# Two-layer graph attention: layer 1's first chunk in two parts of columns, a 13-operation epilogue, and the last chunk of layer 0 finished in GpSimd's order

## What is computed

```python
# layer 0: E are the 64-wide entity embeddings
scores = (x @ W0 @ a1)[:, None] + (E @ W0 @ a2)[None, :]
e = where(adj > 0, leaky(scores, 0.2), -9e15)
x = layernorm(x + elu(softmax(e, axis=1) @ E + x))
# layer 1: the same mask, and the new x is key and value too
wh = x @ W1
e = where(adj > 0, leaky((wh @ a_src)[:, None] + (wh @ a_dst)[None, :], 0.01), -1e9)
x = layernorm(x + softmax(e, axis=1) @ wh + bias)
```

## Time and profile before

| | |
|---|---|
| median of 3 runs | 660.34 us (659.3 to 661.42) |
| the profiled execution: its own time, its span | 659.63 us, 657.8 us |
| mean granted TensorE clock over the span | 0.961 |
| busy share of the span, TensorE matmul / VectorE / ScalarE / GpSimd | 79% / 86% / 79% / 29% |

### The profile page before, as it was taken

How to read it: one execution, slowest core, us unless ns; L and a number is a source line. 1 busy time by engine, 2 the same in 40 slices (tenths; PEclk the granted TensorE clock), 3 DMA queues, 4 the chain that set the end, 5 groups by cost and what they waited for, 6 DMA issues and landing times.

```text
span 657.8 us, 14211 instructions
## 1 busy us (share of the span) xinstructions
PE 517.0 (79%) x6034; PEld 230.6 (35%) x6035; DVE 567.6 (86%) x727; ACT 516.8 (79%) x593; POOL 188.1 (29%) x144
## 2 busy tenths in 40 slices
...
DVE  3898988999899898888467889989998998899685
ACT  0856998899999996988676318979997899699673
...
PEclk9999999999999899999999757999999999999997
...
GB/s 156 326 352 338 292 298 207 273 255 251 158 259 275 249 119 288 130 130 2 73 2 19 1 33 1 1 33 1 1 10 33 1 1 33 1 1 18 1 17 9
DMA packets 18631, 76.46 MB, mean 116 GB/s; under 512 B 6552, under 2 KB 8776, under 8 KB 10376
## 3 DMA queue, kind: packets, MB, share of 16 engines
...
q0 software_dynamic: 256, 0.80, 0.5%
...
q10 hardware_dynamic: 752, 0.13, 0.1%
...
## 4 chain that ended last, share of the span: by engine, by line
PE 28%; DVE 23%; ACT 21%; issue 18%; DMA 5%; POOL 4%; SPq 1%; POOLq 0%; ACTq 0%; DVEq 0%
ACT Pm L620 15%; PE acc L940 15%; DVE junk L726 11%; PE zps L983 8%; DVE zps L820 8%; DMA adj_in<-in_adj 5%; PE acc L947 4%; ACT zps L612 2%; ACT v L513 2%; SPq L354 1%; POOL tAB L412 1%; ACT u_row L529 1%; DVE tot L761 0%; POOL rstd L471 0%; POOL o L409 0%
## 5 line engine op out<-in xcount | busy, mean ns | idle before, releaser
L620 ACT ACTIVATE Pm<-zps,ebias 128x1024 f32<-128x1024 f32 (+1 forms) x320 | 293.4, 933 | 77.0 <-DVE zps L820 67.9
L726 DVE CUSTOM_DVE_ANT_0 junk<-v,u_row 128x2048 int8<-128x2048 int8 (+3 forms) x136 | 305.4, 2266 | 3.3 <-ACT v L513 3.2
L983 PE MATMUL zps<-D,v 128*128 128x128 bf16 x2048 | 173.7, 225 | 55.8 <-DVE D L748 28.7
L983 PEld LDWEIGHTS zps<-D,v 128*128 128x128 fp8e4 x2048 | 118.8, 99 | 216.5 <-ACT zps L612 92.0
L820 DVE SCALAR_TENSOR_TENSOR zps<-S_row,tau_col,zps 128x1024 f32<-128x1024 f32 (+1 forms) x135 | 141.2, 1052 | 52.4 <-PE zps L983 49.6
L612 ACT ACTIVATE zps<-S_row,ntau_col 128x1024 f32<-128x1024 f32 (+1 forms) x185 | 177.4, 959 | 5.4
L940 PE MATMUL acc<-Pm,X 128*32 128x512 f32 (+2 forms) x1280 | 146.5, 530 | 21.4 <-ACT Pm L620 18.1
L940 PE MATMUL acc<-Pm,VE 128*32 128x512 f32 (+2 forms) x1280 | 147.9, 535 | 15.7 <-ACT Pm L620 7.8
L402 POOL TENSOR_TENSOR tAB<-flag,totW 128x520 f32<-128x520 f32 (+1 forms) x8 | 11.1, 1388 | 300.8 <-ACT totW L539 160.9
L947 PE MATMUL acc<-Pm,ones 128*32 128x256 f32 (+1 forms) x1280 | 87.5, 346 | 0.0
L947 PEld LDWEIGHTS acc<-Pm,ones 128*32 128x32 f32 x1280 | 43.3, 114 | 71.4 <-issue 62.0
...
## 6 DMA issues: line engine op xcount, KB each, us to landing
...
```

Source lines behind the costliest of these rows:

```text
L620: a.activation(Pm[:, k % PB, 0:R(C) * P], zps[:, buf("step", k), 0:R(C) * P], ACT.Exp, bias=ebias[:, int(seeded(k)), J:J + 1])\
L726: d.tensor_tensor_reduce(out=junk[:, at % 2, 0:cols.stop - cols.start], in0=v_bytes[:, rt, cols], in1=u_row[:, cols], scale=1.0, scalar=-3 ...
L983: last = t.matmul(zps[:, buf("step", k), r * P:(r + 1) * P], v[:, chunks[C][1] + r, J * P:(J + 1) * P], D[:, C % 2, r, :], start=(r * P % ...
```

## The change

**Two parts of columns.** Chunk 5 (`NC`) now runs its steps 0 to 27 with a diagonal and constants that know only the first 28 column tiles, which chunks 0 to 3 of layer 0 produce. Steps 28 to 31 use a second diagonal, made during chunk 5 from chunk 4's new rows. The two parts have sums of their own in `acc`, are projected apart, and are weighed and added in chunk 5's epilogue. Layer 1's constants come from bounds on the scores (norms of the weight vectors, worked out in chunk 0) in place of the measured extremes.

```diff
+    KNOWN = JT - WIDTHS[0][-1]
+    SPREAD = (NC - 2, NC - 1)
...
+                second = C == NC and J >= KNOWN
+                first, end = J == KNOWN * second, J == JT - 1 or (C == NC and J == KNOWN - 1)
...
+            def second_diagonals():
+                row_terms(NC, slice(len(segments(NC)) - 1, len(segments(NC))))
+                write_diagonals(NC, PART)
+                link(d.tensor_copy(g_parts[:, 1, :], g8[:, 0:PART]))
+                link(d.tensor_tensor(um_known[:, :], um_known[:, :], um8[:, 0:PART], ALU.max))
+                write_flags(NC, um_known[:, :])
+                link(d.tensor_tensor(g_least[:, :], g_parts[:, 0, :], g_parts[:, 1, :], ALU.min))
...
+            if C == NC:
+                eng.wait_ge(weights_done, 1)
+                link(ns.tensor_tensor(o[:, 0:2 * n, :], o[:, 0:2 * n, :],
+                                      part_weight[:, :].unsqueeze(2).broadcast_to([P, 2 * n, F1]), ALU.mult))
+                link(ns.tensor_tensor(o[:, 0:n, :], o[:, 0:n, :], o[:, n:2 * n, :], ALU.add))
```

```diff
-SEEDS = ((29, 28, 28, 16, 12), (28, 18, 18, 10, 0))
+SEEDS = ((29, 28, 28, 16, 26), (26, 18, 18, 10, 0))
...
-    SAVE_ACC, PROJECT, SAVE_O, TOTALS_W, RECIPROCAL = 1, 3, 4, 5, 7
-    AFTER_WIDE = dict(elu=11, sums=14, squares=18, scores=24, rows=26)
-    AFTER_LAST = dict(elu=10, sums=13, squares=17, scores=21, rows=22)
-    IN_LAYER_1 = dict(sums=14, squares=19)
+    SAVE_ACC, PROJECT, SAVE_O, TOTALS_W = 1, 3, 4, 5
+    AFTER_WIDE = dict(reciprocal=7, elu=10, sums=13, squares=17, scores=22, rows=25)
+    IN_LAST = dict(reciprocal=6, elu=9, sums=13, squares=17, scores=21, rows=23)
...
+    IN_FIRST = dict(reciprocal=6, elu=8, sums=10, squares=13, scores=15, rows=17, maxima=19, second=21)
+    IN_LAYER_1 = dict(reciprocal=7, sums=13, squares=18)
...
+    EARLY = (4, 5, 7, 8, 9, 10, 11, 12, 14, 15, 18, 19, 22, 24)
...
-                if C == NC - 1:
-                    for n in range((Q - 2) * R(NC), (Q - 1) * R(NC)):
-                        row_max(NC, n, n % R(NC), n // R(NC))
-                    epilogue(dve, d, link, C, sums, squares, None, scores)
-                    dve.wait_ge(uS_ready, NC + 1)
-                    ext_out(EXT_BOTH)
-                    u_diagonals(uS[:, 0, 0:R(C)], R(C))
-                    ext_max(EXT_BOTH)
-                    ext_in(EXT_BOTH)
-                    t_scalars(1)
-                    s_scalars(1)
-                    for n in range((Q - 1) * R(NC), Q * R(NC)):
-                        row_max(NC, n, n % R(NC), n // R(NC))
-                    diagonals(NC)
```

```diff
-                ns.tensor_scalar(tAf, tBf, 0.0, -3.0e38, ALU.min, ALU.max).then_inc(min_done, 1)
-                eng.wait_ge(min_done, C + 1)
-                link(ns.tensor_tensor(tBf, tBf, tAf, ALU.subtract))
+                ns.tensor_tensor(tBf, h, xs, ALU.add).then_inc(elu_in, 1)
+                eng.wait_ge(negative_done, C + 1)
+                link(ns.tensor_tensor(tBf, tBf, tAf, ALU.add))
                 link(ns.tensor_tensor(tBf, tBf, xs, ALU.add))
                 eng.wait_ge(elu_done, C + 1)
-                link(ns.tensor_scalar(h, h, 1.0, -1.0, ALU.mult, ALU.add))
```

**The scores of chunks 3 and 4** are made from products that VectorE takes itself:

```diff
+                if C in SPREAD:
+                    xs = X[:, xc, 0:F]
+                    per_feature = [wbc[:, k, :].unsqueeze(1).broadcast_to([P, R(C), F]) for k in (2, 3)]
+                    dve.wait_ge(new_done, C + 1)
+                    d.tensor_tensor(tA[:, 0:R(C), 0:F], xs, per_feature[0], ALU.mult).then_inc(sprod_done, 1)
+                    d.tensor_tensor(tB[:, 0:R(C), :], xs, per_feature[1], ALU.mult).then_inc(tprod_done, 1)
```

More of the change, by code:

```diff
@@ L198, in written, with segments @@
         def written(event):
-            return 32 * min(event, NC - 1) + 16 * (event == NC)
-        def early(q):
-            n = chunks[NC - 1][1]
-            if q == Q - 1:
-                return slice(n * P, N)
-            return slice(q * n // (Q - 1) * P, (q + 1) * n // (Q - 1) * P)
-        def u_of(q):
-            return [c for c in range(NC) if early(q).start < rows(c).stop and rows(c).start < early(q).stop]
+            return 32 * min(event, SPREAD[0]) + 16 * max(event - SPREAD[0], 0)
+        def segments(C):
+            if C == NC:
+                first_spread = rows(SPREAD[0]).start
+                ends = [0, first_spread // 2, first_spread, KNOWN * P, N]
+            elif C == NC + 1:
+                ends = [0, QW, KNOWN * P, N]
+            else:
+                ends = [0, QW, N]
+            return [slice(a, b) for a, b in zip(ends, ends[1:])]
         users = []
@@ L379, in _, with epilogue @@
                     store_out(C - 1)
-            store_out(NCH - 1)
-            sp.wait_ge(out_written, stored(NCH - 1))
-        def epilogue(eng, ns, link, C, sums=None, squares=None, inverse=None, scores=None):
+            store_out(LAST)
+            sp.wait_ge(out_written, stored(LAST))
+        def epilogue(eng, ns, link, C, sums=None, squares=None, inverse=None):
             n = R(C)
@@ L703, in compare, with bounds @@
+            def bounds():
+                dve.wait_ge(bound_done, 1)
+                g = bound[:, 1:2], bound[:, 1:2], bound[:, 0:1]
+                link(d.tensor_scalar(uoff[:, 1:2], bound[:, 1:2], 1.0, None, ALU.add))
+                t_scalars(1, g)
+                s_scalars(1, g)
             def compare(H):
```

459 lines of the change are left out of this document (271 added, 188 removed).

## The result

The changed kernel takes 657.38 us, the median of 4 runs (656.58 to 657.54), the kernel before on the same chip 660.54 (659.3 to 661.42). The ratio is 0.9954, 95% interval 0.9942 to 0.9967: faster, by 3.2 us by the medians (3.0 by the ratio) and not by the 9.5 that I forecast.

What follows compares the result with a forecast made beforehand. It took the handover as bound by latency, chunk 5 by row maxima, chunk 4 as having room. From 659.6 us, -12.5 + 1 + 1 + 1.5 - 0.5 = -9.5 gave 650.1, stated as 650.5; range 641 to 659.

Steps and rivals of the forecast that it cites:

- the handover: Between chunk 4's last product and chunk 5's first turn: 22.9 us, of which VectorE's 19.3 would leave the path.
- The moves of the steps by one or two cost nothing, hidden by row maxima.: Epilogue operations placed one or two steps differently: priced at no cost, as row maxima would hide the moves.
- the stretch: From chunk 4's first exponential to chunk 6's first: 114.6 us before, forecast 102, a gain of 12.5.
- my +1 for the Relu: Chunks 1 to 3: ScalarE gets one Relu each, 0.4 or 0.65 us, with no room in chunk 2: +1 us.
- My fallback, 2 us in each chunk: If the moved steps are not hidden by row maxima, a wait of 2 us comes back in each chunk.
- The row maxima ... one costs 2.2 us: VectorE's row maxima: 2.2 us per piece of 2048 columns, 28.8 us for chunk 4's 26,624 columns.
- GpSimd's own 18 us for chunk 4's epilogue: 11 GpSimd operations in chunk 4, half taken as slowed by row maxima: 18 us, VectorE waiting about 3.
- Chunk 5, 50 us: Chunk 5, from its first exponential to chunk 6's: about 50 us; much different would mean the prediction is wrong.
- ScalarE, 83.2 us: ScalarE's work in chunks 4 and 5: exponentials and seeds 76.2 us, copies 4 and 3; over 85% busy.
- The longest waits at steps 24, 25 and 18: ScalarE's longest waits would be at VectorE's operations at steps 24 and 25 of chunk 4 and 18 of chunk 5.
- the crawl rival: GpSimd at its slow end beside row maxima in chunks 4 and 5: 654 to 658 us; chance 0.14.
- The slower rival: Chunk 4's epilogue, 11 operations all at 2.7 us, holds TensorE at chunk 5's step 17: 662 to 666; chance 0.08.

Runs made afterwards that it cites:

- e1: Changed kernel with the epilogue's steps in chunks 1 to 3 put back to their old places (ELU, sums, squares, scores, rows): 653.3 us.
- e5: e1 with VectorE in place of GpSimd taking the mean off and squaring for the epilogues of chunks 3 and 4: 652.7 us.
- e12: e5 with chunk 3's rows at step 25 of chunk 4 in place of 23, and two row maxima moved from chunk 4 to chunk 5: 655.54 us.
- e7: Kernel before with only the 13-operation epilogue added, old steps and old handover: 661.0 us, ratio 0.9993.
- e9: Changed kernel with only the rows' step in chunks 1 to 3 put back from 25 to 26: 656.49 us.
- e10: Changed kernel with the scores' step (24) and the rows' step (26) in chunks 1 to 3 put back: 656.62 us.
- e4: Changed kernel with GpSimd's operations of chunk 3's epilogue, which runs in chunk 4, on one row tile of eight (power unchanged): 650.8 us.

## Why the prediction was wrong

The direction and the mechanism of the gain held: the handover's work left the path. The size did not: two terms of the sum were wrong, one priced at nothing without a reason that held, the other without the wait for GpSimd. (By its own terms my sum came to 650.1 and 0.7, 650.8; I wrote 650.5.)

- **"The moves of the steps by one or two cost nothing, hidden by row maxima."** This failed. Shown by e1: 4.1 us by the medians, 3.8 by the ratios. It is about all of the 4.4 us that were lost ahead of the stretch (with the old table chunk 4's first exponential is at 321.28, 322.89 and 322.32 in e1, e5 and e12, 322.19 before). My +1 for chunk 0 turned out as nothing (its end at 104.78, was 104.91), and my +1 for the Relu is no more than that in e7's profile, 323.16 where 322.19 was. My fallback, 2 us in each chunk, was near for chunk 3 alone (2.2; it is 1.0 in chunk 2 and nothing clear in chunk 1), and the scores' step, of whose wait I had thought, is worth nothing by e9 and e10. The rows' step is worth 1.9 us by e9; through which wait stays open.
- **"The row maxima ... one costs 2.2 us" (28.8 us in chunk 4).** This failed, and it is the whole miss of the stretch. Chunk 4 took 56.9 us, not 51.3. The 26,624 columns took 35.4 us. Alone the pieces would have durations of 8 x 1.44 + 6 x 2.29 + 4 x 1.22 = 30.1, where they have 36.1: 6.0 us are the wait for GpSimd's operations. My 28.8 is right for the pieces alone, with their overlaps counted once; it left out this wait. With GpSimd's operations cut to an eighth, e4 has 31.1 (30.4 us busy) and chunk 4 takes 50.3, 1 us below the forecast. I had priced what VectorE does to GpSimd and not what GpSimd does to VectorE, although a row of before had a trace of it: eight row maxima of 1152 columns averaged 1.53 us there, more than the 1.44 that 1280 columns take (in that trace they run from 1.35 to 2.07 us).
- **GpSimd's own 18 us for chunk 4's epilogue.** Right in size: 16.1 us, mean 1.46 for 11 operations, below the 2 us that I had named. VectorE waited for it at the sums for 3.34 us (I said 3), and for 1.59 more at the scores' products.
- **Chunk 5, 50 us.** Right: 50.2 (383.46 to 433.62), VectorE 39.7 us of work (I said 40.7).
- **ScalarE, 83.2 us.** About right: 43.7 + 36.9 = 80.5. These are the windows from `D` to `D`. It was not over 85% busy in either, 74% and 79%.
- **The longest waits at steps 24, 25 and 18.** Wrong place. ScalarE's wait is at step 23, 8.84 us, because TensorE stood behind the scores for 7 us. This is the wait that the crawl rival named ("4 to 5 us in place of 2"), and its stretch of 106 to 109 holds the measured 107.1. Its place for chunk 5's start, 376 (+4.4 for what stood ahead: 380), was still 3 us early. That its 654 to 658 holds the measured time too is in part luck: without the steps' 4.1 us, which it did not have, the time is e1's 653.3. My own sign of being wrong, chunk 4 beyond 376, came true: chunk 5 starts at 383.46.
- **The clock stays near 1.0.** Wrong: 0.88 and 0.85 in chunks 4 and 5. The hole before had 0.57 over 22.9 us, so the long hole in it is gone, but TensorE's waits for the scores brought two short stretches at the half level: 366.5 to 369.0 in chunk 4, and 411 to 416 in chunk 5 (granted clock 0.50), after 5 us in which TensorE was busy for 1.5. Chunk 5 had 0.87 before.
- **Chunks 6 to 9 and the end.** +0.8 us for +1.0. Right in size. Chunk 6 took 63.6 us.
- **The slower rival** needed GpSimd at 2.7 us for each operation in chunk 5. Six of them took 1.9 to 2.5 us and five 0.6 to 0.7, three of these in VectorE's wait at the sums, as I had argued.

By the runs, the change is three parts: the 13-operation epilogue 0, the new handover -6.3 us by the ratios of e1 and e7 (-7.7 by their medians), the earlier steps about +4. The best version measured is e5, 652.7 us, with e1 not told apart from it by time.

What stays open: why rows at 26 beside the early ELU make chunk 1 2 us longer, by which wait rows at 25 lengthen chunk 3, and why the power leaves the row maximum beside it as short as one alone.
